# Two Fourier layers on one core: layer 1's second matmul in column tiles of 64, and Re minus Im formed by GpSimd ahead of layer 0's first matmul

## What is computed

```
# layer 0
f  = fft2(x);  Xh = f.real - f.imag                    # first 23 kw are kept
o1 = relu(Xh @ w1[0] + b1[0]);  o2 = o1 @ w2[0] + b2[0]
x  = ifft2(softshrink(o2, 0.01)).real + x
# layer 1
xf = rfft2(x);  xr, xi = xf.real, xf.imag               # first 23 kw are kept
o1r = relu(xr @ w1[0] - xi @ w1[1] + b1[0]);  o1i = relu(xi @ w1[0] + xr @ w1[1] + b1[1])
o2r = softshrink(o1r @ w2[0] - o1i @ w2[1] + b2[0]);  o2i = softshrink(o1i @ w2[0] + o1r @ w2[1] + b2[1])
y  = irfft2(o2r + 1j * o2i) + x
```

## Time and profile before

| | us |
|---|---|
| median of 3 runs (lowest to highest) | 551.11 (551.05 to 554.34) |
| the profiled execution | 549.69 |
| its span, first to last instruction | 547.9 |
| PE busy | 506.0 |
| VectorE busy | 305.5 |
| ScalarE busy | 210.9 |
| GpSimd busy | 135.6 |

### The profile page before, as it was taken

One profiled execution on the slowest core, in us unless ns is written; L12 is line 12 of the kernel. 1 busy time (PEld: TensorE's weight loads), 2 busy tenths in 40 slices (PEclk: granted clock), 3 DMA queues, 4 the chain that ended last, 5 costly groups with the idle time before them and its releaser, 6 DMA issues.

```text
span 547.9 us, 14234 instructions
## 1 busy us (share of the span) xinstructions
PE 506.0 (92%) x5824; PEld 372.7 (68%) x5824; DVE 305.5 (56%) x675; ACT 210.9 (38%) x473; POOL 135.6 (25%) x146
## 2 busy tenths in 40 slices
PE   4559999999999999999999999999999999999763
PEld 1147777767777777777777777777777777887521
DVE  6414455456754667456763577456764577556643
ACT  0015544553344433554245433444345434343201
POOL 9701211012330132212331133211331111111124
PEclk9759999999999999999999999999999999999978
DMA  8869764576889578886889588886889655633388
GB/s 184 260 155 245 204 173 109 112 206 173 237 214 239 147 192 246 212 203 173 251 200 228 156 205 237 220 200 168 249 202 220 178 159 150 152 95 101 107 222 252
DMA packets 76717, 104.60 MB, mean 191 GB/s; under 512 B 7761, under 2 KB 63303, under 8 KB 76526
## 3 DMA queue, kind: packets, MB, share of 16 engines
q1 hardware_dynamic: 57622, 55.97, 38.9%
q0 software_dynamic: 10608, 40.45, 28.4%
q10 hardware_dynamic: 8424, 7.28, 5.2%
HBM read 52.23 MB, written 51.43 MB: 189 GB/s over the span
## 4 chain that ended last, share of the span: by engine, by line
PE 84%; DVE 5%; DMA 3%; POOL 3%; ACT 2%; issue 2%; SPq 0%; POOLq 0%; ACTq 0%; DVEq 0%
PE ps L666 15%; PE ps L599 13%; PE ps L566 11%; PE ps L692 11%; PE ps L653 11%; PE ps L612 9%; PE ps L630 7%; PE ps L679 5%; PE ps L641 3%; DVE img L545 2%; DMA scr_f<-fs 2%; DVE ns L519 1%; POOL img L379 1%; ACT p L435 1%; POOL xs L362 1%
## 5 line engine op out<-in xcount | busy, mean ns | idle before, releaser
L545 DVE TENSOR_TENSOR img<-ps,img 90x768 f32<-90x768 f32 x92 | 82.7, 900 | 21.7 <-PE ps L599 17.0
L362 POOL TENSOR_TENSOR xs<-xs,nt 128x360 f32<-128x360 f32 (+1 forms) x48 | 41.5, 864 | 212.1 <-DVE nt L497 134.2
L599 PE MATMUL ps<-jr,cst 64*128 64x384 f32 (+1 forms) x358 | 82.5, 528 | 6.7 <-DVE img L545 5.9
L666 PE MATMUL ps<-wt,o 128*109 128x96 f32 (+1 forms) x768 | 85.4, 263 | 0.1
L666 PEld LDWEIGHTS ps<-wt,o 128*109 128x109 f32 (+1 forms) x768 | 76.4, 171 | 13.3 <-issue 12.5
L519 DVE SCALAR_TENSOR_TENSOR ns<-p,ps 109x384 f32<-109x384 f32 x96 | 53.1, 553 | 57.2 <-ACT p L435 57.2
L566 PE MATMUL ps<-img,cst 128*64 128x384 f32 (+1 forms) x368 | 74.0, 520 | 11.4 <-DMA img<-x 7.6
L612 PEld LDWEIGHTS ps<-cst,bt 128*64 128x64 f32 x1472 | 63.2, 141 | 20.6 <-issue 13.9
L371 POOL DMA_DIRECT2D y<-img x42 | 34.7, 827 | 170.7 <-DVE img L545 170.7
L428 ACT ACTIVATE o<-ps,wt 97x180 f32<-97x180 f32 (+1 forms) x96 | 33.8, 406 | 108.8 <-PE ps L653 108.8
L612 PE MATMUL ps<-cst,bt 128*64 128x90 f32 x1472 | 69.0, 248 | 6.3 <-DMA bt<-scr_f 6.3
(11 more groups left out here) (43 smaller groups left out, 411.9 us busy)
## 6 DMA issues: line engine op xcount, KB each, us to landing
y<-img POOLq DMA_DIRECT2D x35, 540.0 KB, 5.1
img<-x POOLq DMA_DIRECT2D x30, 540.0 KB, 8.3
scr_i<-et SPq DMA_DIRECT2D x48, 270.0 KB, 5.8
scr_f<-fs SPq DMA_DIRECT2D x176, 72.0 KB, 3.0
bt<-scr_f SPq DMA_DIRECT2D x40, 270.0 KB, 4.6
jr<-scr_i SPq DMA_DIRECT2D x48, 216.0 KB, 5.3
img<-x ACTq DMA_DIRECT2D x10, 540.0 KB, 6.7
y<-img SPq DMA_DIRECT2D x11, 270.0 KB, 3.6
```

Source lines behind the costliest of these rows:

```text
L362: nc.gpsimd.tensor_tensor(re, re, nt[s % 2][:, :, 0:kws(s), 0:H], ALU.subtract).then_inc(re_ok, 1)
L545: nc.vector.tensor_tensor(y, p, y, ALU.add).then_inc(i_add, 1)
L599: last = mm(ps[:, B0 + r, 0:n], K["w_inv"][64 * r:64 * r + 64, :], set_rows(t, j)[64 * r:64 * r + 64, at, 0:n], start=True, stop=True)
L666: last = mm(ps[0:rows, P2 + p, b * 2 * BS:(b + 1) * 2 * BS], o11[:, b, 2 * p:2 * p + kw, :].rearrange("p k m -> p (k m)")[:, 0:rows], w21[ ...
```

## The change

- `c0`: GpSimd forms `xd` = real minus imaginary of `xs` once per step, at the entry `a` of its list (semaphore `re_minus_im`, `xd_ok` in the code). `c0` then has four matmuls with `w10` on `xd`, with no accumulation, and waits for `xd_ok` in place of the two copies of `a`. The negated weights and the VectorE instruction that made them go. Before, GpSimd waited for the copies of `a` at its entry `d0`; this wait moves to the entry `a`.
- `d1`: each matmul with both `kw` of a pair as stationary operand becomes two, one for each `kw` (`r`), with 64 stationary columns each, to output partitions `64*r` to `64*r + 63`.

```diff
+        xd = sb("xd", [128, 2, STEP * H])
@@ gpsimd
-                if kind == "d0":
+                if kind == "a":
                     s, = what
                     pool.wait_ge(a_act, s + 1)
                     pool.wait_ge(a_dve, s + 1)
+                    xt = xs[s % 2][:, :, 0:kws(s), :]
+                    nc.gpsimd.tensor_tensor(xd[:, :, 0:kws(s) * H].rearrange("p q (k m) -> p q k m", m=H), xt[:, :, :, 0:H], xt[:, :, :, H:2 * H],
+                                            ALU.subtract).then_inc(xd_ok, 1)
+                if kind == "d0":
+                    s, = what
                     pool.wait_ge(d0_ss, 2 * s + 2)
@@ vector
-                    nc.vector.tensor_scalar(w10[1][:], w10[0], -1.0, None, ALU.mult).then_inc(w_ok, 1)
@@ tensor, c0
-                    pe.wait_ge(a_act, s + 1)
-                    pe.wait_ge(a_dve, s + 1)
+                    pe.wait_ge(xd_ok, s + 1)
...
-                    for im in range(2):
-                        for ab in range(2):
-                            for q in range(2):
-                                k = slice(64 * ab, 64 * ab + 64)
-                                last = mm(ps[64 * q:64 * q + 64, P1 + ab, 0:n], w10[im][k, f, q, :], xt[k, q, 0:kws(s), im * H:(im + 1) * H],
-                                          start=im == 0, stop=im == 1)
+                    for ab in range(2):
+                        for q in range(2):
+                            k = slice(64 * ab, 64 * ab + 64)
+                            last = mm(ps[64 * q:64 * q + 64, P1 + ab, 0:n], w10[k, f, q, :], xd[k, q, 0:n], start=True, stop=True)
@@ tensor, d1
-                        rows = 64 + H if kw == 2 else H
                         for b in range(4):
-                            last = mm(ps[0:rows, P2 + p, b * 2 * BS:(b + 1) * 2 * BS],
-                                      o11[:, b, 2 * p:2 * p + kw, :].rearrange("p k m -> p (k m)")[:, 0:rows],
-                                      w21[:, block_no(s // STEPS, b), :], start=True, stop=True)
+                            for r in range(kw):
+                                last = mm(ps[64 * r:64 * r + 64, P2 + p, b * 2 * BS:(b + 1) * 2 * BS], o11[:, b, 2 * p + r, :],
+                                          w21[:, block_no(s // STEPS, b), :], start=True, stop=True)
```

More of the change, by code:

```diff
@@ L170, in spectral_layers @@
             at += m
-        w10 = [V["w10"].rearrange("p (f q o) -> p f q o", f=HALVES, q=2), sb("w10_neg", [128, HALVES, 2, 64])]
+        w10 = V["w10"].rearrange("p (f q o) -> p f q o", f=HALVES, q=2)
         w20 = V["w20"].rearrange("p (f q o) -> p f q o", f=HALVES, q=2)
@@ L206, in spectral_layers @@
         a_mm, a_act, a_dve = sem("a_product"), sem("a_copied_act"), sem("a_copied_dve")
+        xd_ok = sem("re_minus_im")
         c0_mm, c0_act, c0_dve = sem("c0_product"), sem("c0_relu_act"), sem("c0_relu_dve")
@@ L477, in _ @@
                     nc.vector.tensor_scalar(v, v, LAM, None, ALU.add).then_inc(w_ok, 1)
-                    dve.wait_ge(w_ok, 5)
+                    dve.wait_ge(w_ok, 4)
                 if kind == "a":
@@ L616, in _ @@
                     s, = what
-                    n, f, xt = kws(s) * H, s // STEPS % HALVES, xs[s % 2]
+                    n, f = kws(s) * H, s // STEPS % HALVES
                     if s == 0:
-                        pe.wait_ge(w_ok, 5)
-                    pe.wait_ge(a_act, s + 1)
-                    pe.wait_ge(a_dve, s + 1)
+                        pe.wait_ge(w_ok, 4)
+                    pe.wait_ge(xd_ok, s + 1)
                     if s > 0:
```

## The result

The changed kernel takes 526.74 us (median of 4 runs, 525.56 to 528.73) against 552.54 us for the kernel before (4 runs, 551.05 to 554.34): 0.9535 of its time, 95% interval 0.9485 to 0.9586. Forecast were 526.5 us and a range of 520.5 to 537.0. The profiled execution took 527.67 us, its span is 525.8.

A forecast was written before the change was run, and what follows sets the result against it. TensorE, busy for 92% of the span, was taken as the bound. From 549.69 us, -14.0 (`c0`), -11.2 (`d1`) and +0.4 twice (start) gave 525.3; 526.5 was stated for the median, range 520.5 to 537.

The forecast's parts named there:

- TensorE's list is the bound: Mid-kernel, TensorE runs its list end to end, so cuts there shorten the kernel: 14.0 us from `c0`, 11.2 from `d1`.
- `d1` in the step of three `kw`: `d1` where the second half has one `kw`: 1.47 to 1.66 us, 1.47 taken, 0.25 saved a step, 2.0 in all.
- The subtraction is hidden: GpSimd's subtraction before `c0`: 0.89 us, ceiling 1.8, off the path in ordinary steps, 1.8 us to spare in the tightest.
- The start: Steps 0 and 1: the subtraction delays `c0`, +0.4 us each; a later full clock could add up to 2 us.
- Waits behind `d0` stay as they are: TensorE's waits at `t` and `c1` on VectorE and GpSimd work that starts from `d0` would not change.
- The sum: Whole kernel: -14.0 (`c0`), -11.2 (`d1`), +0.4 and +0.4 (start) make -24.4 us, so 525.3 for the profiled execution.
- `d1` gains nothing: Rival at `d1`: twice as many loads to issue cancel its gain, 538 us; chance 0.08.
- Time comes back as other waits: Rival mid-kernel: DMA loads land later against an earlier TensorE, a third of the gain returns, 535 us; chance 0.10.
- The slower rival by loads of halves that take turns: Rival at `d1`: column halves load and multiply in turn, loss from 0.116 us a pair, 619 us; slower rivals together 0.04.

The follow-up runs named there:

- c0_only: Changed kernel with `d1` put back as it was, so only the subtraction and the shorter `c0` remain; 537.20 us, 0.9715 of the kernel before.
- before_two_waits: Kernel before, without GpSimd's two waits for the copies of `a` ahead of the addition; 552.58 us in one run.
- both_again: Changed kernel unaltered, run again on the chip of a version with the subtraction on VectorE; 525.33 us, 0.9521 of the kernel before.
- after: Changed kernel unaltered, in its profiled execution; 527.67 us, with a median of 526.74 us over 4 runs.
- both: Changed kernel unaltered, run again beside its two halves; 526.89 us, 0.9531 of the kernel before.
- d1_only: Kernel before with only the new `d1` loop, `c0` as before and no subtraction on GpSimd; 539.32 us, 0.9781 of the kernel before.
- d1_grouped: Changed kernel with `d1`'s matmuls reordered, per `kw` pair four blocks for one column half, then four for the other; 546.64 us.

## Why the prediction was right

- *TensorE's list is the bound.* Right. Priced from start to start, 47 `c0` ahead of a `d1` went from 35.7 to 21.8 us (13.9; forecast 14.0 with step 0 apart) and all 48 `d1` from 83.3 to 71.8 (11.5, of which 0.2 are a single `d1` that took 1.90 us in the trace of before; forecast 11.2). The analogies did it: `c0` behaves as `d0`, the new `d1` as `a` plus 6 columns, 1.47 us to the hundredth, where the change of tile shape on both sides had to be counted.
- *`d1` in the step of three `kw`*: 1.47 forecast out of 1.47 to 1.66, 1.46 in each of seven. Single instructions of one half go at 0.083 us, no slower than a pair.
- *The subtraction is hidden.* Right, by the one wait in 48 steps. Its price was 0.82, not 0.89. But the tightest step was not the one that the prediction priced at 1.8 us of slack (1.97 there in the changed kernel). It counted the load that GpSimd issues ahead of the subtraction in step 1 alone; steps 2 to 6 have it too, and in steps 5 and 6, which have neither `fwd` nor `inv` to cover it, 1.31 and 0.84 us were left. At 0.82 us for the subtraction this cost nothing; at the prediction's ceiling of 1.8, step 6 would have waited.
- *The start.* +0.4 and +0.4 were forecast. Step 0 waits 1.79 us in place of 0.79 and `c0` costs 0.6 less: +0.4, right. In step 1 the subtraction ended at 42.29 and did not hold `c0`: `c1` ahead of it took from 40.59 to 42.76, 2.17 us in place of 1.53, because the clock came later. In `c0_only` the subtraction did hold it, by 0.3 us. That the longer idle time delayed the clock, which the prediction left to the range, is not shown: `before_two_waits`, which has no subtraction, needs 2.03 us for the same `c1`, and `both_again` 2.65. And the shorter `c0` of step 1 gains nothing (0.98 us to `d1`, before 0.99): `d1` waits 0.45 us for the ReLU of `c1` (43.75 in the rows on the start of the pipeline). The prediction looked at the ReLUs that `d0` needs, not at those that `d1` needs. The amount (+0.6 for `c1` and 0.3 not gained, for +0.4) is off by half a microsecond. The stretches of `c1` of step 0 (PE and the others busy, then clock, DMA share), after and before:

```profile
40.60:42.76 2.16, 2.16 (x16) 1.89 (x17) 0.53 (x1) 0.00 (x0) 1.67 (x2) 0.63 1.02 226
```

```profile
40.70:42.23 1.53, 1.53 (x16) 1.30 (x16) 0.53 (x1) 0.00 (x0) 0.85 (x1) 0.90 0.93 218
```

- *Waits behind `d0` stay as they are.* Not quite: `c1` starts 0.15 us sooner in the seven steps in which it waits for the addition, 1.1 us in all, because two waits left GpSimd's list ahead of the addition. I had not priced them.
- *The sum* for the profiled execution was 525.3 and it took 527.67, 2.4 more. The first `c0` starts 0.5 us later than before, and from there to the last `d1` the trace has 24.2 us less. The rest is behind: from the last `d1` to the end it takes 35.9 us in place of 34.3, though the change has nothing there. PE's clock in it, by stretch (PE busy and so on, clock, DMA share), after:

```profile
498.30:509.90 11.60, 7.72 (x22) 3.67 (x24) 4.17 (x5) 0.60 (x1) 1.79 (x3) 0.56 0.84 207
```

and before, for the same entries:

```profile
522.26:533.00 10.74, 6.87 (x22) 3.18 (x22) 4.17 (x5) 0.58 (x1) 1.79 (x3) 0.68 0.89 223
```

PE works longer at 1.2 GHz there. The tail goes with the clock that was granted in it: 35.9 us at a mean of 0.78 in `after`, 34.3 at 0.83 in before, 34.2 at 0.83 in `both`, 33.5 at 0.86 in `both_again`. So two us of it differ from one execution to the next. The medians of the runs are 25.8 us apart, where the sum was 24.4; that the median of 526.74 came within 0.3 us of the 526.5 stated is luck, since this profiled execution missed its sum by 2.4 and the kernel before has a median of 552.54 over four runs where the prediction had 551.11 over three.
- *The rivals.* `d1` gains nothing: out by `d1_only`. Time comes back as other waits: nearly out. Apart from the 0.45 us of step 1, PE's waits that recur from step to step did not grow, and none on DMA joined them. One came through ScalarE: in the middle its copies of `fwd` waited 9.0 us for earlier stores to `scr_f` to land (10.4 in `both`), 6.3 in the kernel before, and once PE waited 0.8 us for such a copy (0.5 in `both`). The 0.8 us once ahead of `c1` (`issue` in the waits of `after`) come and go: `both` has 1.8, `before_two_waits` 1.5 ahead of a `c0`. The slower rival by loads of halves that take turns: out by `d1` at 1.47 us with 32 loads and 32 matmuls, a pair every 0.083 us where 0.116 was the point of loss. A rule of the Trainium skill ("TensorE: Matmul & The Clock Gate", the section on packing small matmuls) is that a load overlaps matmuls in flight only across row groups. The traces disagree: column halves on the same rows overlap too, 1.38 us of loads beside 1.54 us of matmuls in the `d1` at 43.7. In `d1_grouped` matmuls of the later half even started ahead of earlier ones of the first half.

## What to carry to other kernels

Where one engine is busy from end to end, price an edit from the starts of neighbouring entries, and look for work of the same tile shape with the same neighbours; a new tile shape that the trace already holds elsewhere gave its cost here to the hundredth of a microsecond. For small matmuls ask which operand sets the pace: here a stationary operand wider than the moving one (109 against 96) was better cut into column halves that alternate, and with a moving operand wider than it (128) the cut was worth almost nothing. Work that is moved to an idle engine costs nothing only up to the cover behind it; look for the step with the least cover by what stands ahead of the work in that engine's list. Beyond the cover it costs more than its own wait, since what stands behind it in that list becomes late too.

## What the runs showed of the hardware

- The pace of fp32 matmuls of 128 rows: 0.096 us an instruction with 109 stationary and 96 moving columns, 0.083 with 45 or 64 stationary ones, 0.109 with 128 moving columns and 45 to 109 stationary ones; 0.083 for a pair of 64-column halves with 96 moving columns, +0.23 us for 16 instructions when the 109-column form moves 128, +0.43 for 16 pairs.
- TensorE starts matmuls out of the order of its list when they go to another column half: `d1_grouped` costs 1.96 us, not the 2.8 of one after another.
- Two more semaphore waits ahead of a GpSimd instruction, both met long before, delay it by 0.14 us behind the wait that ends last (0.23 against 0.09).
- fp32 subtraction of 128x360 from SBUF to SBUF: 0.82 us on GpSimd, 0.62 on VectorE. The addition of layer 0's result, which the code makes as a subtraction of `nt` with the output in place of an input, takes 0.89 on GpSimd.
